# Second attention of a two-attention decoder: maxima subtracted through stack rows, stack halves between spill stages, residual biases later

## Chip, cores and metric

The kernel runs on one core of one Trainium2 chip. The metric is the device time of one execution in microseconds (us). Engines are named as in the profile: PE (TensorE matmul), PEld (its weight loads), DVE (VectorE), ACT (ScalarE), POOL (GpSimd), SP (SyncE); SPq and ACTq are the DMA issues of SP and ACT.

## What is computed

One decoder layer over 16 batches of 128 tokens, width 128, 16 heads of 8 features, post-norm: a first attention with a decayed second score term and mixed values, a layer norm, a second attention whose keys and values come from a context, a layer norm, and a mixture of 16 experts (top 4) with a last layer norm. The part that the change touches:

```python
Q = query @ Wq.T + bq; K = key @ Wk.T + bk; V = value @ Wv.T + bv
energy = jnp.einsum('bhqd,bhkd->bhqk', Q, K) / jnp.sqrt(jnp.float32(HD))
attn = jax.nn.softmax(energy, axis=-1)
x = jnp.einsum('bhqk,bhkd->bhqd', attn, V)
return x.transpose(0, 2, 1, 3).reshape(b, -1, D) @ Wo.T + bo
```

## The kernel before

Every stage works batch by batch. To get float32 scores out of bf16 matmuls, queries and keys are cut into three bf16 parts (`high` and `middle` on ACT, L1216 and L1220; `remainder` and `lowest` on POOL, L498 and L504). SP **spills** the parts to DRAM (L365, L369, L370, L373) and loads them back **stacked** (L396, `stack2`): one bf16 operand holds the 48 part-by-feature rows that a head needs, on the even partitions 0 to 94, for all 16 heads, once for the queries (side 0) and once for the keys (side 1). The other partitions hold zeros. There are four such stacks (`stk2`), laid over the two stacks `stk` of the first attention.

A batch of the second attention then goes through these steps, four heads (a group) at a time. `score2` (L799, four bf16 matmuls) makes scores with the queries in the rows. `maximum2` on DVE (L1529) takes each query's maximum over the keys into `top`. When all 16 heads are done, `turn_top` (L812) transposes `top` into bank 6 and ACT copies it into `top_t`, one row per head (`take_top`, L1245). `score_t` (L821) makes the scores again with the keys in the rows, and four more bf16 matmuls (L828) subtract the maxima from them:

```python
m = pe.matmul(bank[2 + g % 2][:, 128 * j:128 * j + 128],
              neg_ident[:, h:h + 1].broadcast_to([128, 128]), top_t[:, b.par, :],
              start=False, stop=True, skip_group_check=True)
```

ACT exponentiates (`exponent2`, L1236), PE weighs the values (`weigh`, L844), transposes to tokens (`to_tokens`, L857), DVE divides (L1536, L1542), PE turns (L866) and multiplies by the output weights (`out_product`, L870) with ACT's copy between them (`take_out`, L1261), DVE adds residual and bias (`residual`, L1560), takes the moments (L1548 to L1553) and normalises (`norm_out`, L1566) with a power from POOL (L578). The bias of the residual is added to x ahead of time, four batches in one POOL instruction (`residual_bias`, L641).

The order is written out by hand. A **slot** is four units g = 0 to 3; in PE's slot n, unit g does in this order: for g = 0 `project2` of batch n+3 (L751, L752), one group of `score2`, one of `score_t` (batch n-2), at g = 1 and 3 a `weigh`, at g = 1 `turn_out` and at g = 2 `out_product` (batch n-4), at g = 2 `turn_top` (batch n-1), at g = 3 `to_tokens` (batch n-3). ACT, DVE, POOL and SP have the same slots with their own steps. Slots 0 to 3 of the second attention overlap the last steps of the first; in them `last_slot1` gives POOL the first attention's layer norms (`gain_and_sum`, `inverse_root`). In slots 12 to 17 the routing of the first 8 batches is added (`route_first` on PE, `route_stage` on DVE). Slot n starts where `project2` of batch n+3 runs. The experts follow and end at 355.4 us.

Each engine's queue is in order. A step waits for semaphores: `score2` for the stack (`stacked`) and the maximum two groups back (`maxed`), `score_t` for the exponent two groups back (`exped`), `exponent2` for the subtraction (`shifted`), SP's `stack2(b)` for its spill and for the last subtraction of batch b-4, which used the same stack.

## Time and profile before

| | us |
|---|---|
| median of 3 runs (lowest to highest) | 356.3 (355.46 to 356.36) |
| the profiled execution, its own time | 357.19 |
| its span, first to last instruction | 355.4 |
| PE busy, share of the span | 326.9 (92%) |
| DVE busy | 250.7 (71%) |
| POOL busy | 215.4 (61%) |
| ACT busy | 190.7 (54%) |
| mean busy share of the 16 DMA engines by queue: SP's, ACT's | 51.9%, 0.9% |

The profiled execution took 1.8 us more than its span, and stands 0.9 us over the median. Busy is the time in which an engine had an instruction of its own; register, semaphore and DMA-issuing instructions are not counted. A busy share over the whole span says little here, since the stages have different limits; the stage is to be read by itself, in stretches of time and in the order of its instructions. In a timeline row stand the start, the duration, the engine, the line, the operation, out<-in with the shapes, the count of merged instructions, and in brackets the idle time just before with what ended it. The TensorE clock was granted at 0.995 of full speed on average.

### The profile page before, as it was taken

How to read it: one execution, taken by the hardware profiler on the slowest of the kernel's cores; microseconds unless marked ns; L12 is line 12 of the kernel's file. 1: busy time of each engine (PE TensorE's matmuls, PEld its weight loads, DVE VectorE, ACT ScalarE, POOL GpSimd, SP SyncE). 2: the span in 40 equal slices, each digit the busy share in tenths (PEclk: the TensorE clock that was granted, in tenths of full speed). 3: DMA queues.
4: the chain of work that ended last, by engine and by line, in shares of the span. 5: the costliest groups of instructions: out<-in, count | busy, mean ns of one | idle time of the engine just before them, and what ended most of it. 6: DMA issues, size and time to landing. Idle time of an engine off the chain costs nothing.

```text
span 355.4 us, 11656 instructions
## 1 busy us (share of the span) xinstructions
PE 326.9 (92%) x3728; PEld 259.1 (73%) x3728; DVE 250.7 (71%) x1220; ACT 190.7 (54%) x458; POOL 215.4 (61%) x402
## 2 busy tenths in 40 slices
PE   6989899998999999975799999998889999999993
PEld 3877788887888888864588887887646765666662
DVE  1688899988989999966367767769754279254454
ACT  3586566766676665575677767754643342222220
POOL 8375899998889977788733343311134445554552
PEclk9999999999999999999999999999999999999998
DMA  7669797775677688545454544641055300624310
GB/s 219 191 188 307 233 268 229 231 223 166 202 201 208 179 235 236 168 130 140 115 133 115 145 116 99 164 106 46 10 175 183 87 32 7 180 88 144 122 32 30
DMA packets 67808, 54.07 MB, mean 152 GB/s; under 512 B 29617, under 2 KB 57649, under 8 KB 67633
## 3 DMA queue, kind: packets, MB, share of 16 engines
q1 hardware_dynamic: 67328, 52.43, 51.9%
q10 hardware_dynamic: 432, 1.05, 0.9%
q8 instruction: 25, 0.41, 0.5%
q14 instruction: 23, 0.18, 0.2%
HBM read 33.40 MB, written 20.05 MB: 150 GB/s over the span
## 4 chain that ended last, share of the span: by engine, by line
PE 45%; POOL 16%; issue 11%; DVE 9%; DMA 9%; ACT 4%; SPq 4%; POOLq 0%; ACTq 0%; DVEq 0%
PE bank L844 6%; PE bank L1109 5%; DMA parts_dram<-parts 4%; PE bank L1113 4%; PE bank L784 4%; PE bank L1122 4%; DMA stk<-parts_dram 2%; PE bank L773 2%; POOL rstd L562 2%; PE bank L799 2%; POOL rest L498 2%; DMA sup_w<-in_sup_w_dram 2%; PE bank L828 2%; PE bank L821 2%; PE bank L787 2%
## 5 line engine op out<-in xcount | busy, mean ns | idle before, releaser
L707 POOL TENSOR_TENSOR stk<-stk 128x512 f32<-128x512 f32 x32 | 40.8, 1274 | 38.3 <-ACT stk L1434 35.4
L1227 ACT ACTIVATE prob_t<-bank 128x512 f32<-128x512 f32 x64 | 38.7, 605 | 41.6 <-PE bank L787 41.6
L1518 DVE CUSTOM_DVE_ANT_0 sums<-bank,decayed_e 128x128 f32<-128x128 f32 x256 | 59.1, 287 | 0.7
L1529 DVE TENSOR_REDUCE top<-bank 128x4 bf16<-128x512 f32 x64 | 43.9, 687 | 17.2 <-PE bank L799 16.9
L1236 ACT ACTIVATE prob_t<-bank 128x512 f32<-128x512 f32 x64 | 38.8, 606 | 26.7 <-PE bank L828 26.3
L1774 DVE TENSOR_TENSOR stk<-bank,stk 128x512 f32<-128x512 f32 x32 | 22.0, 691 | 39.2 <-POOL stk L707 38.0
L1434 ACT ACTIVATE stk<-bank 128x512 f32<-128x512 f32 x32 | 19.1, 597 | 53.6 <-PE bank L1109 53.6
L1506 DVE TENSOR_TENSOR decayed_e<-bank,decay 128x512 f32<-128x512 f32 x64 | 44.0, 687 | 2.5 <-issue 1.9
L498 POOL TENSOR_TENSOR rest<-pf,parts 128x256 f32<-128x256 f32 (+1 forms) x31 | 28.1, 908 | 28.9 <-ACT parts L1216 28.8
L844 PE MATMUL bank<-prob_t,vmix 128*32 128x128 f32 x1024 | 42.6, 278 | 2.2 <-ACT pvs L1253 2.2
L784 PE MATMUL bank<-ident,sums 128*128 128x128 f32 x256 | 39.3, 276 | 2.7 <-ACT prob_t L1227 1.2
L504 POOL TENSOR_TENSOR parts<-rest,parts 128x256 bf16<-128x256 f32 (+1 forms) x31 | 28.2, 908 | 20.5 <-ACT parts L1220 20.5
L1122 PEld LDWEIGHTS bank<-w,stk 128*128 128x128 f32 x192 | 25.1, 191 | 11.9 <-issue 8.4
L1109 PE MATMUL bank<-x_t,w 128*128 128x512 f32 x64 | 32.9, 595 | 0.0
L1113 PE MATMUL bank<-x_t,w 128*128 128x512 f32 x64 | 32.7, 592 | 0.0
L844 PEld LDWEIGHTS bank<-prob_t,vmix 128*32 128x32 f32 x1024 | 25.7, 109 | 9.4 <-issue 3.9
L784 PEld LDWEIGHTS bank<-ident,sums 128*128 128x128 f32 x256 | 28.0, 141 | 5.8 <-DVE shift L1518 3.5
L763 PE MATMUL bank<-stk 128*128 128x128 bf16 x256 | 24.8, 219 | 1.2 <-DMA stk<-parts_dram 1.2
L1122 PE MATMUL bank<-w,stk 128*128 128x128 f32 x192 | 25.4, 275 | 0.0
L799 PE MATMUL bank<-stk 128*128 128x128 bf16 x256 | 24.9, 220 | 0.4 <-DVE top L1529 0.4
L773 PE MATMUL bank<-stk 128*128 128x128 bf16 x256 | 25.0, 220 | 0.0
L821 PE MATMUL bank<-stk 128*128 128x128 bf16 x256 | 24.8, 219 | 0.0
(171 smaller groups left out, 756.6 us busy)
## 6 DMA issues: line engine op xcount, KB each, us to landing
stk<-parts_dram SPq DMA_DIRECT2D x32, 384.0 KB, 4.3
stk<-shares_dram SPq DMA_DIRECT2D x64, 128.0 KB, 2.9
parts_dram<-parts SPq DMA_DIRECT2D x32, 192.0 KB, 3.5
parts_dram<-parts SPq DMA_DIRECT2D x48, 128.0 KB, 3.1
stk<-parts_dram SPq DMA_DIRECT2D x32, 192.0 KB, 2.9
parts_dram<-parts SPq DMA_DIRECT2D x32, 96.0 KB, 2.3
parts_dram<-parts SPq DMA_DIRECT2D x48, 64.0 KB, 2.1
w<-in_w_dram SPq DMA_DIRECT2D x3, 512.0 KB, 5.6
```

The lines of the kernel that those rows point to most:

```text
L498: pool.tensor_tensor(rest[:, :, L.kinds, :], pf[:, :, L.kinds, :], by_part[b.par][:, HIGH, L.kinds, :], ALU.subtract).then_inc(L.rest, 1)
L707: pool.tensor_tensor(h1[kk % 2], sg[kk % 2], share[kk], ALU.mult).then_inc(weighted, 1)
L784: pe.matmul(bank[3][:, 128 * j:128 * j + 128], sums[g % 2][:, j, :], ident[:], start=(j == 0), stop=True, is_transpose=True, skip_group_ch ...
L844: w = pe.matmul(bank[4][32 * j:32 * j + 32, 128 * m:128 * m + 128], vmix[b.par][:, head(2 * m, j) // 2, e:e + 2, :].rearrange("p e f -> p ...
L1109: pe.matmul(bank[kk % 2][:], w1[:, 128 * kk:128 * kk + 128], xt, start=True, stop=True).then_inc(gate_mm, 1)
L1113: pe.matmul(bank[UP_BANK[u % 3]][:], w3[:, 128 * kk:128 * kk + 128], xt, start=True, stop=True).then_inc(up_mm, 1)
L1122: m = pe.matmul(bank[4 + c % 2][:, 128 * t:128 * t + 128], actt[u % 3][:, 128 * t:128 * t + 128], w2[:, kk, :], start=(kk == 0 and t == 0) ...
L1227: act.activation(prob_t[g][:].rearrange("p h t -> p (h t)"), bank[3][:], ACT.Exp).then_inc(L1.exped, 1)
L1236: act.activation(prob_t[g][:].rearrange("p h t -> p (h t)"), bank[2 + g % 2][:], ACT.Exp).then_inc(L2.exped, 1)
L1506: dve.tensor_tensor(decayed_e[:, g % 2], bank[E_BANK[g % 2]][:].rearrange("p (h t) -> p h t", h=GH), decay[:].unsqueeze(1).broadcast_to([1 ...
L1518: m = dve.tensor_tensor_reduce(out=sums[g % 2][:, j, :], in0=bank[g % 2][:, 128 * j:128 * j + 128], in1=decayed_e[:, g % 2, j, :], scale=1 ...
L1529: dve.tensor_reduce(top[:, b.par, GH * g:GH * g + GH], bank[S2_BANK[g % 2]][:].rearrange("p (h t) -> p h t", h=GH), AX.X, ALU.max).then_in ...
```

## The change

**Rows for the maxima.** The stacks have unused partitions. Rows 96 to 111 of the key side now hold, for head h, minus one in row 96+h and zero in the others (`pick_rows`, two DMAs early in the program; the number in the constant is one whose float32 bits are two bf16 of -1). Rows 96 to 111 of the query side hold all 16 maxima, put there for every head by a DMA that ACT issues (`top_rows`, 16 partitions of 16 copies of 128 bf16, 64 KB). So the four matmuls of `score_t` subtract the maxima too, and those of L828 are gone. `score2` of the next batch in the same stack needs zeros in these rows: POOL clears them (`clear_row`, 16 partitions of 1024 float32), for the 12 batches that have a successor in their stack.

**Order.** `score2` and `maximum2` run three units earlier. `turn_top` moves from unit 2 to unit 3 of the slot before, into bank 4, and `take_top` to ACT's unit 0; `top_rows` follows the exponent of unit 0. SP loads a stack in two halves of 8 heads, both sides in one DMA; a half waits for half of batch b-4's `score_t`, and the halves stand between the three stages of the next batch's spill. `clear_row(b)` opens POOL's slot b+3. The residual biases move from the transition (slots 0 to 3) to the ends of slots 3, 5, 7 and 9. Loops of SP, POOL and DVE over the slots are written out.

```diff
+            def pick_rows(p):
+                sp.wait_ge(zeroed[p], 1)
+                keys = stk[p][:].rearrange("p a h u t -> p (a h u t)").bitcast(F32)[TOP_ROW:TOP_ROW + H, H * S:2 * H * S]
+                sp.dma_start(keys.rearrange("p (k n) -> p k n", k=2),
+                             k["pick_rows"].unsqueeze(1).broadcast_to([H, 2, H * S // 2])).then_inc(in_rows_k, 16)
...
-                for side in range(2):
-                    sp.dma_start(stk2[b.buf][0:2 * R:2, side], src[side]).then_inc(L2.stacked[b.buf], 16)
+                if half == 0:
+                    sp.wait_ge(L2.spilled[b.par], b.pair * L2.spill_step + L2.spill_step)
+                if b.n >= 4:
+                    sp.wait_ge(L2.shifted, NG * b.n - 4 * NG + NM + NM * half)
...
+            for s in range(NB - 2):
+                if s + 3 < NB:
+                    spill_high(L2, slot_batch(s + 3))
+                stack2(slot_batch(s + 2), 0)
+                if s + 3 < NB:
+                    spill_mid(L2, slot_batch(s + 3))
+                stack2(slot_batch(s + 2), 1)
+                if s + 3 < NB:
+                    spill_low(L2, slot_batch(s + 3))
...
+            def clear_row(b):
...
+                pool.wait_ge(L2.shifted, NG * b.n + NG)
+                pool.memset(stk2[b.buf][TOP_ROW:TOP_ROW + H, 0].rearrange("p h t -> p (h t)").bitcast(F32), 0.0
+                            ).then_inc(L2.row_zero, 1)
...
+                c = b.back(3)
+                if c.live and c.n < NB - 4:
+                    clear_row(c)
+                    pool.wait_ge(L2.row_zero, c.n + 1)
...
+            for n in range(1, NB + 4):
+                if n < 4:
+                    last_slot1(NB + 1 + n, None)
                 slot2(slot_batch(n))
+                if n % 2 == 1 and 3 <= n < 11:
+                    residual_bias(2 * n - 6, 2 * n - 2)
...
             def score_t(b, g):
...
+                if g == 0:
+                    pe.wait_ge(L2.topped[b.par], b.pair * 16 + 16)
                 for j in range(GH):
-                    pe.matmul(bank[2 + g % 2][:, 128 * j:128 * j + 128], stk2[b.buf][:, 1, head(g, j), :],
-                              stk2[b.buf][:, 0, head(g, j), :], start=(j == 0), stop=True,
-                              skip_group_check=True)
-                if g == 0:
-                    pe.wait_ge(L2.top_t_ev, b.n + 1)
-                for j in range(GH):
-                    h = GH * g + j
-                    m = pe.matmul(bank[2 + g % 2][:, 128 * j:128 * j + 128],
-                                  neg_ident[:, h:h + 1].broadcast_to([128, 128]), top_t[:, b.par, :],
-                                  start=False, stop=True, skip_group_check=True)
+                    m = pe.matmul(bank[2 + g % 2][:, 128 * j:128 * j + 128], stk2[b.buf][:, 1, head(g, j), :],
+                                  stk2[b.buf][:, 0, head(g, j), :], start=True, stop=True)
...
-                sb_, sg_ = unit_back(bb.back(1), g, -2)
+                sb_, sg_ = unit_back(bb.back(1), g, -5)
...
-                if g == 2 and bb.back(1).live:
-                    turn_top(bb.back(1))
+                if g == 3 and bb.live and (not isinstance(bb.n, int) or bb.n >= 1):
+                    turn_top(bb)
...
+            def top_rows(b):
+                act.wait_ge(L2.top_t_ev, b.n + 1)
+                act.dma_start(stk2[b.buf][TOP_ROW:TOP_ROW + H, 0],
+                              top_t[0:H, b.par, :].unsqueeze(1).broadcast_to([H, H, S])).then_inc(L2.topped[b.par], 16)
...
-                if g == 3 and bb.back(1).live:
+                if g == 0 and bb.back(1).live:
                     take_top(bb.back(1))
...
                 if bb.back(2).live:
                     exponent2(bb.back(2), g)
+                if g == 0 and bb.back(1).live:
+                    top_rows(bb.back(1))
```

The line numbers of the two programs differ: after the change `score2` is L843, `score_t` L865, `weigh` L885, `out_product` L911, the exponent L1283, the row DMA L1288, the clearing L696, the stack L422.

PE, units 2 and 3 of slot 5 (banks 0 and 5 take `score2`, 2 and 3 `score_t`). Before:

```order
L799 MATMUL bank0<-stk1 128x128 [waits maxed2,stacked21]
L799 MATMUL bank0<-stk1 128x128 x3
L821 MATMUL bank2<-stk1 128x128 [waits exped2]
L821 MATMUL bank2<-stk1 128x128 x3
L828 MATMUL bank2<-top_t,neg_ident 128x128 x4
L870 MATMUL bank7<-late_w,attn_ot 128x128 [waits o_t_ev2]
L812 MATMUL bank6<-ident_bf,top 16x128 [waits top_t_ev2,proj_ev2,maxed2]
L799 MATMUL bank5<-stk1 128x128 [waits maxed2]
L799 MATMUL bank5<-stk1 128x128 x3
L821 MATMUL bank3<-stk1 128x128 [waits exped2]
L821 MATMUL bank3<-stk1 128x128 x3
L828 MATMUL bank3<-top_t,neg_ident 128x128 x4
```

Now, the same two units:

```order
L843 MATMUL bank5<-stk1 128x128 [waits maxed2]
L843 MATMUL bank5<-stk1 128x128 x3
L865 MATMUL bank2<-stk1 128x128 [waits exped2]
L865 MATMUL bank2<-stk1 128x128 x3
L911 MATMUL bank7<-late_w,attn_ot 128x128 [waits o_t_ev2]
L843 MATMUL bank0<-stk0 128x128 [waits maxed2,row_zero2,stacked24]
L843 MATMUL bank0<-stk0 128x128 x3
L865 MATMUL bank3<-stk1 128x128 [waits exped2]
L865 MATMUL bank3<-stk1 128x128 x3
```

Two groups of L828 are gone from these two units and four from the slot; the first group of a new batch stands in unit 3, where it waits for the cleared row and for the first half of its stack, and the transpose stands behind the `weigh` that follows these rows.

ACT, from the exponent of unit 0 to `take_out` in unit 1, inside its loop. Before:

```order
L1236 ACTIVATE prob_t0<-bank2 128x512 [waits pv2]
L1193 ISA
L1198 ACTIVATE pf<-bank6,bias_q 128x128 [waits rest2,proj_done2]
L1201 ACTIVATE pf<-bank6,first_w 128x128
L1231 REGISTER_ALU
L1236 ACTIVATE prob_t1<-bank3 128x512 [waits pv2,shifted2]
L1211 ISA
L1215 REGISTER_ALU [waits proj_ev2]
L1216 CAST parts0<-pf 128x2x128 [waits spilled20]
```

Now:

```order
L1296 COPY top_t<-bank4 16x128 [waits topped20]
L1278 ISA
L1280 ISA [waits shifted2]
L1283 ACTIVATE prob_t0<-bank2 128x512 [waits pv2]
L1288 DMA stk0<-top_t 16x16x128 [waits top_t_ev2]
L1240 ISA
L1245 ACTIVATE pf<-bank6,bias_q 128x128 [waits rest2,proj_done2]
L1248 ACTIVATE pf<-bank6,first_w 128x128
L1278 REGISTER_ALU
L1283 ACTIVATE prob_t1<-bank3 128x512 [waits pv2,shifted2]
```

The copy of the maxima has moved ahead of the slot's first exponent, and a DMA issue stands between that exponent and the projection.

SP, one slot's worth. Before, one stack and then one whole spill:

```order
L396 DMA stk1<-parts2_dram 48x2048 x2
L365 DMA parts2_dram<-parts0 128x3x128 x2
L369 DMA parts2_dram<-parts0 128x2x128
L370 DMA parts2_dram<-parts0 128x2x128
L373 DMA parts2_dram<-parts0 128x2x128
```

Now:

```order
L376 DMA parts2_dram<-parts1 128x3x128 x2
L422 DMA stk0<-parts2_dram 48x2x1024
L384 DMA parts2_dram<-parts1 128x2x128
L385 DMA parts2_dram<-parts1 128x2x128
L422 DMA stk0<-parts2_dram 48x2x1024
L392 DMA parts2_dram<-parts1 128x2x128
```

Seven issues have become seven; the stack of one batch is threaded between the stages of the next batch's spill.

## Rows read from the trace of the kernel before

**Rows 1.** Stretches: us; busy PE, PEld, DVE, ACT, POOL; clock, DMA share, GB/s

```profile
154.70:177.20 22.50, 14.98 (x219) 12.09 (x216) 12.45 (x38) 14.35 (x39) 18.83 (x46) 1.00 0.49 119
177.72:183.46 5.74, 5.70 (x92) 4.71 (x91) 3.86 (x11) 4.44 (x12) 1.94 (x3) 1.00 0.42 103
217.86:223.67 5.81, 5.70 (x93) 4.70 (x91) 4.20 (x13) 4.06 (x12) 2.08 (x4) 1.00 0.46 120
223.67:229.59 5.92, 5.92 (x96) 5.08 (x95) 4.21 (x13) 4.49 (x13) 2.08 (x4) 1.00 0.67 163
229.59:236.78 7.19, 7.19 (x109) 6.37 (x107) 4.33 (x13) 3.55 (x9) 2.02 (x4) 1.00 0.49 122
235.00:259.60 24.60, 21.88 (x355) 17.93 (x354) 19.18 (x75) 12.41 (x29) 3.69 (x8) 1.00 0.19 54
```

**Rows 2.** Timeline of PE, from the start of slot 7 to that of slot 8

```profile
194.93 0.39 PE L751 MATMUL bank<-x_t,late_w 128*128 128x128 f32 x2
...
195.60 0.39 PE L821 MATMUL bank<-stk 128*128 128x128 bf16 x4
...
195.82 0.39 PE L828 MATMUL bank<-top_t,neg_ident 128*128 128x128 bf16 x4
...
198.44 0.49 PE L870 MATMUL bank<-late_w,attn_ot 128*128 128x128 f32 x2
...
198.86 0.22 PE L812 MATMUL bank<-ident_bf,top 128*16 128x128 bf16 x1
...
200.66 0.39 PE L751 MATMUL bank<-x_t,late_w 128*128 128x128 f32 x2
```

**Rows 3.** Timeline of ACT in the same slot: first exponent, copy for the output product

```profile
196.32 0.60 ACT L1236 ACTIVATE prob_t<-bank 128x512 f32<-128x512 f32 x1 [1.27 <-PE bank L828]
...
198.09 0.30 ACT L1261 COPY attn_ot<-bank 128x128 f32<-128x128 f32 x1
```

**Rows 4.** Timelines of POOL, DVE and PE in the transition, slots 2 to 4

```profile
164.79 1.27 POOL L641 TENSOR_TENSOR xb_all<-x_tok,rows 128x512 f32<-128x512 f32 x1
...
167.04 0.29 DVE L1596 BATCH_NORM_STATS2 stats<-res 128x6 f32<-128x128 f32 x1 [2.27 <-POOL res L573]
...
167.98 0.22 PE L812 MATMUL bank<-ident_bf,top 128*16 128x128 bf16 x1 [2.24 <-DVE top L1529]
...
177.23 0.66 PE L1001 MATMUL bank<-ident,x_tok 128*128 128x128 f32 x4 [0.92 <-ACT x_tok L1272]
```

**Rows 5.** Timeline of DVE, slots 14 to 17: ends of its full stretch

```profile
237.20 0.69 DVE L1529 TENSOR_REDUCE top<-bank 128x4 bf16<-128x512 f32 x1 [2.04 <-PE bank L799]
...
254.45 0.39 DVE L1745 TENSOR_TENSOR shares<-vsz,rsm 128x128 f32<-128x128 f32 x1
```

**Rows 6.** The page, DMA issues: KB each, median us from issue to landing

```profile
stk<-parts_dram SPq DMA_DIRECT2D x32, 192.0 KB, 2.9
...
parts_dram<-parts SPq DMA_DIRECT2D x48, 64.0 KB, 2.1
```

**Rows 7.** SP's stack of L396: landings of all, and one issue of two DMAs

```profile
DMA to landing us min/median/max: 2.7/2.9/4.3
...
201.06 1.29 SPq L396 DMA_DIRECT2D stk<-parts_dram  x2
```

**Rows 8.** Start of the program: POOL clears both stacks, ACT issues a DMA

```profile
0.73 6.96 POOL L483 MEMSET stk<- 128x4096 f32 x2 [0.29 <-POOLq L1903]
...
1.66 0.45 ACTq L1190 DMA_DIRECT2D x_t<-in_x_t_dram  x1
```

**Rows 9.** DVE's normalisation alone in slot 7, and beside a POOL instruction later

```profile
197.49 0.34 DVE L1566 TENSOR_SCALAR c_tok<-res,mv,rstd 128x128 f32 x1
...
263.39 1.26 POOL L707 TENSOR_TENSOR stk<-stk 128x512 f32<-128x512 f32 x1
...
263.46 1.28 DVE L1566 TENSOR_SCALAR c_tok<-res,mv,rstd 128x128 f32<-128x128 f32 x1 [0.18 <-POOL rstd L578]
```

More of the change, by code:

```diff
@@ L236, in __init__ @@
                 self.spilled = [sem(f"spilled{n}{p}") for p in range(2)]
-                self.stacked = [sem(f"stacked{n}{p}") for p in range(4)]
+                self.stacked = [sem(f"stacked{n}{p}") for p in range(4 * n)]
                 self.ent_scores = sem(f"ent_scores{n}")
@@ L323, in build @@
         RT_STEPS = 22
+        TOP_ROW = 96
         WARM = 10
@@ L350, in load_ffn, with spill_places @@
                 sp.dma_start(w2[:].rearrange("p c n -> p (c n)"), k["w2"]).then_inc(in_ffn, 16)
-            def spill(L, b):
+            def spill_places(L, b):
                 if L is L1:
@@ L406, in _ @@
             spill(L1, Batch(0, 0))
-            sp.wait_ge(zeroed[0], 1)
+            pick_rows(0)
             stack1(Batch(0, 0), 0)
@@ L410, in _ @@
             spill(L1, Batch(0, 1))
-            sp.wait_ge(zeroed[1], 1)
+            pick_rows(1)
             stack1(Batch(0, 1), 0)
@@ L425, in _ @@
             pair1(NB // 2 - 1)
-            def quad2(q):
-                for i4 in range(4):
-                    b = Batch2(q, i4)
-                    stack2(b)
-                    if b.back(-1).live:
-                        spill(L2, b.back(-1))
-            spill(L2, Batch2(0, 0))
-            load_ffn()
-            quad2(0)
-            with sp.Fori(1, 3) as q:
-                quad2(q)
-            quad2(3)
+            spill(L2, slot_batch(0))
+            load_ffn()
+            spill(L2, slot_batch(1))
+            stack2(slot_batch(0), 0)
+            stack2(slot_batch(0), 1)
+            spill(L2, slot_batch(2))
+            stack2(slot_batch(1), 0)
+            stack2(slot_batch(1), 1)
+            for s in range(NB - 2):
[7 more added lines that the diff above has]
+                    spill_low(L2, slot_batch(s + 3))
             def spill_shares(half):
@@ L906, in unit2 @@
                     project2(bb.back(-3))
-                sb_, sg_ = unit_back(bb.back(1), g, -2)
+                if g == 0 and isinstance(bb.n, int) and bb.n == 0:
+                    score2(bb, 0)
+                sb_, sg_ = unit_back(bb.back(1), g, -5)
                 if sb_.live:
                     score2(sb_, sg_)
+                if g == 0 and isinstance(bb.n, int) and bb.n == 1:
+                    turn_top(bb.back(1))
                 tb = bb.back(2)
@@ L1065, in route_first @@
                     turn_shares(0, 1)
+            pe.wait_ge(in_rows_k, 16)
             first_slot()
+            pe.wait_ge(in_rows_k, 32)
             pair1(1)
@@ L1647, in unit2 @@
                     residual(L2, bb.back(4), TAIL2)
-                sb_, sg_ = unit_back(bb.back(1), g, -2)
+                if n == 0 and g == 0:
+                    maximum2(bb, 0)
+                sb_, sg_ = unit_back(bb.back(1), g, -5)
                 if sb_.live:
@@ L1751, in scan @@
                 rstep(dve.tensor_tensor(r[dst][:, :, sh:NE], r[src][:, :, sh:NE], r[src][:, :, 0:NE - sh], ALU.add))
-            dve.wait_ge(xb2, 1)
-            slot2(slot_batch(4))
-            dve.wait_ge(xb2, 4)
-            with dve.Fori(1, 3) as q:
-                for i4 in range(1, 5):
-                    slot2(Batch2(q, 0).back(-i4))
-            for n in range(13, NB + 3):
+            for n in range(4, NB + 3):
                 slot2(slot_batch(n))
@@ L1895 @@
                                    v["L0_ffn_gate_w"].T], 1),
+        "pick_rows": _np.repeat(-1.0058441162109375 * _np.eye(H), S // 2, 1),
         "x_t": turned(v["x"]),
```

113 lines of the change are left out of this document (61 added, 52 removed).

## The prediction, made blind

> **What bounds the kernel now.** I read the stretches first (busy time of each engine by stage), then PE's, ACT's and DVE's timelines in the second attention, and last what SP's queue and its landings leave over.
>
> The stretches [rows 1] show three kinds of stage. In slots 4 to 11 (177.72 to 223.67, eight slots in 45.95 us, 5.74 each) PE is busy 5.70 of 5.74; DVE has 4.2, ACT 4.1, POOL 2.1. PE is the bound there, and slots 12 and 13 (5.92 and 7.19 us) are fully PE's. In the transition (154.70 to 177.20) PE has 15.0 of 22.5 us and POOL 18.8: POOL bounds it, through the first attention's layer norms. In 235.00 to 259.60 DVE has the most work beside the routing, and its timeline has no gap from 237.20 to the end of the shares at 254.84 [rows 5].
>
> Inside a PE slot [rows 2] a group of four bf16 matmuls costs 0.22 us (195.60 to 195.82). The one real wait is before L870: it follows ACT's copy at 198.09 [rows 3] by 0.35. So a second chain is hidden just under PE's: the group of L828 at 195.82, the exponent at 196.32 (0.50 later), ACT's in-order work to the copy at 198.09 (1.77 more), L870 at 198.44, then the rest of PE's slot, 2.22 us to 200.66. This chain closes on itself once per slot, since the next slot's first `score_t` comes behind it on PE.
>
> **The slots 4 to 11.** The change takes four groups of L828 from each slot, 0.89 us of PE work. If PE alone decided, a slot would be 4.85. But only two of the groups lie on the chain: the one before the first exponent (0.22) and the one after L870 (0.22); the other two lie where PE waits for L870 anyhow. Besides, L812 stood 0.42 behind L870 because it waited for DVE's last maximum; it now comes later in the slot, with all maxima three units earlier, which gives some 0.1 back. A slot becomes 5.74 - 0.22 - 0.22 - 0.1 = 5.20.
>
> The DMA that ACT now issues stands inside this chain, between the exponent and the projection. The nearest row is ACT's issue at the start, 0.45 us [rows 8]. Below is nothing: the exponent runs 0.60 us and the next ACT instruction starts 0.5 behind it, so an issue by ACT's sequencer may fit beside it. Above is 0.45. I take 0.1, as the order of the two favours the overlap: slot 5.30, eight slots save 8 x 0.44 = 3.5 us. Bounds: 0.7 (slot 5.65) to 4.3 (5.20).
>
> What covers the rest. *The row DMA* moves 64 KB. It is issued about 1.7 us after the slot's start and needed by the next slot's `score_t`, 0.66 after that starts, so 4.2 us later. The nearest row by size lands in 2.1 us, SP's stacks of 192 KB in 2.9, the slowest in 4.3 [rows 6, 7]. I take 2.1 to 2.9: hidden. The Trainium skill, SBUF — State Buffer, section "Door 1: The DMA port swizzle", says that a transfer's rate depends on the SBUF ports its partitions reach, and gives 16 adjacent partitions 4 ports, about 109 GB/s. By that, an estimate, the 64 KB would take 0.6 us beside the fixed part instead of 0.15, and land near 2.6; the sum stays the same. No row of this trace has so few partitions.
>
> *The clearing* is 1024 elements; POOL cleared 2 x 4096 in 6.96 us, 0.85 us per 1024 [rows 8]. POOL has 3.6 us free per slot, and the row is needed only in unit 3 of that slot: nothing on the path. Four later bias pieces (1.27 each [rows 4]) bring a slot of POOL to 2.1 + 0.9 + 1.3 = 4.3, still under 5.3. But POOL's power, which DVE's normalisation waits for, now stands behind both; DVE has 1 us of slack per slot. I allow nothing, and up to 0.5 in three slots in the range. DVE's normalisation took 0.34 alone and 1.28 where it ran beside a POOL instruction of 1.26 [rows 9]. The Trainium skill, SBUF — State Buffer, section "SBUF: two separate sides", calls the port pair of VectorE and GpSimd an exclusive lock held for the whole instruction; the row agrees. By that rule a normalisation that meets a bias piece loses up to 0.9, in three slots 2.7; by rows it waits for the power behind that piece and so cannot meet it.
>
> *The stacks* are needed three groups earlier. Before, a stack was issued in one piece (1.29 us of SP for the pair, at 201.06 [rows 7]) after the last `score_t` of batch b-4. Now a half needs only half of that batch, which is two units earlier, and does not queue behind a whole spill. With 2.9 us to land, the first half of batch b comes about 1.4 us before unit 3 of slot b-1. DVE's load per slot is unchanged, 4.2 of 5.3.
>
> **The transition.** DVE waited 2.27 us for POOL's sum and PE 2.24 for DVE's maximum [rows 4]. POOL's queue ran full, and three bias pieces, each holding it 1.22, stood ahead of work that DVE waited for: 3.7 us. Against it: the first clearing (0.9) stands in slot 3 ahead of the remainder, whose middle part ACT makes before the last x1 row that PE waits for at 177.23 [rows 4]; and DVE takes three more maxima in slot 0 and `score2` of batch 1 may wait for its stack, some 0.6 together. Net 2.2. Bounds: 0 (another chain of the layer norms takes over) to 3.7.
>
> **Slots 12 to 17.** Slots 12 and 13 keep the same chain and PE's extra work: 0.7 each, 1.4 (bounds 0.8 to 1.8). In slots 14 to 16 DVE is full, so PE's saving is worth nothing there; but three of the ten maxima in the full stretch have moved to slots before it, at 0.6 apiece (0.69 long [rows 5], the next started 0.6 later): 1.8 (1.2 to 2.1). In slot 17 the last batch loses its four groups on the way to the last exponent: 0.5 (0.2 to 0.9).
>
> **The start.** `pick_rows` adds two loads of 128 KB behind the first two spills on SP's queue. Their issue lies in SP's wait for the spill, but the bytes go ahead of the first stacks: 0.4 lost (0 to 1).
>
> **Sum.** 3.5 + 2.2 + 1.4 + 1.8 + 0.5 - 0.4 = 9.0 us less. The profiled execution took 357.19 (span 355.4), so it would take 348.2, with a span of 346.4. The median of the runs is 0.9 lower than that execution: 356.3 - 9.0 = 347.3. The experts after 259.6 only shift.
>
> **Rivals.**
> 1. *The issue counts in full.* ACT's DMA issue does not overlap the exponent: slot 5.65, the eight slots give 0.7 and slots 12 and 13 some 0.4 less: gain 5.8, 350.5 us. For it: ACT's other instruction at the start came right behind its issues. Against: nothing then ran on ACT's datapath. Chance 0.15.
> 2. *The stacks or POOL decide.* SP has seven issues per slot (0.37 to 0.65 each) and a spill's landing of 2.1 between the last issue and the next half, near 5 us, barely under the slot; contention would set the slot at 5.5: 8 x 0.2 less than forecast, and another 1 in slot 0: gain 6.4, 349.9. Chance 0.11. With it go cases where two or three small terms fail together and 353 is reached, 0.04.
> 3. *The rows come late, and it is slower.* The place is `score_t` of unit 0. The loop is: group, exponent 0.5 later, issue 0.5 later, landing L, PE 0.1: slot = L + 1.1. It passes 5.30 at L = 4.2 and the old 5.74 at 4.6. For: the transfer shares the engines with SP's 192 KB halves; the slowest of those took 4.3 [rows 7]; DMA engines are about half busy [rows 1]. Against: the median is 2.9 for three times the bytes. At L = 5.2 the slot is 6.3: slots 4 to 11 lose 8 x 0.56 = 4.5, slot 12 loses 0.4, slot 13 gains 0.7, slots 14 to 16 (16.9 us before) lose 2.0, transition, slot 17 and start keep 2.3: 3.9 slower, 360.2. It decides from L = 4.85. Chance 0.09. The Trainium skill, DMA: Bandwidth & Descriptors, section "Issuing engines are not separate DMA queues", says that DMAs of all engines run on the same 16 and interleave, so ACT's own queue would not shield the rows. This trace has ACT's queue only at the start and cannot show it.
>
> **The numbers.** Forecast 0.61, the rivals 0.15, 0.15 (with the small failures) and 0.09. A measurement of this kernel tells about 0.3%, 1.1 us, from no change. The forecast's own bounds are 343.5 (most terms at their high end: 12.8) to 351 (the issue, the transition and slots 12 to 17 at their low ends); rivals 1 and 2 and the failures reach to 353.5; the late rows are left out. Range 343.5 to 353.5. Faster 0.87, same 0.04, slower 0.09.
>
> **What the new profile would show.** Slots 4 to 11 at 5.2 to 5.4, with PE idle before L911 and its releaser ACT's copy; the idle time before `score_t` (L865) small. ACT's row DMA landing in 2 to 3 us. The projection 0.5 to 0.6 behind the slot's first exponent (rival 1: 0.9 or more). No idle time before L843 on a stack or a cleared row (rival 2). Slot 4 starting at about 175.9, DVE's full stretch about 15.8 long. A PE wait for the row DMA in every slot, or slots near 6, would make the prediction wrong.

## The result, and the profile after

The changed kernel takes 353.94 us (median; 351.20 to 357.83, 20 executions); the kernel before took 357.63 in the executions beside it. The ratio is 0.9881, 95% interval 0.9857 to 0.9904: 4.2 us faster, not 9.0. (Ratios here leave out executions more than 1.5% above the fastest of their kernel, five of the twelve of e11 for one; medians do not, and so the two can differ.) The profiled execution took 354.09 with a span of 352.3, 3.1 less than the 355.4 before. The stretches after, from slot 1 to the experts; the columns are those of [rows 1]:

```profile
157.25:176.52 19.27, 13.65 (x161) 11.21 (x160) 10.31 (x31) 11.76 (x32) 14.65 (x38) 0.88 0.59 147
176.52:182.79 6.27, 5.63 (x75) 4.80 (x75) 3.56 (x10) 4.45 (x12) 2.47 (x4) 0.82 0.40 98
176.52:222.02 45.50, 38.65 (x593) 31.31 (x593) 33.02 (x94) 32.35 (x89) 27.59 (x42) 0.98 0.59 142
222.02:228.02 6.00, 5.57 (x87) 4.59 (x86) 4.47 (x15) 4.72 (x14) 3.26 (x6) 1.00 0.76 174
228.02:234.52 6.50, 5.95 (x86) 5.08 (x84) 4.12 (x12) 3.58 (x8) 3.70 (x6) 1.00 0.44 110
234.52:256.41 21.89, 18.66 (x263) 13.71 (x262) 17.57 (x71) 12.03 (x28) 3.06 (x7) 0.84 0.14 42
```

PE's work fell as planned (38.65 us in slots 4 to 11), but those slots still take 45.50. Against the forecast, by stage:

| stage | before | forecast | after |
|---|---|---|---|
| start of slot 1 | 157.86 | 158.3 | 157.25 |
| slots 1 to 3 | 19.86 | 17.7 | 19.27 |
| slots 4 to 11 | 45.95 | 42.4 | 45.50 |
| slots 12, 13 | 13.11 | 11.7 | 12.50 |
| slot 14 to the experts | 22.84 | 20.5 | 21.89 |
| experts to the end | 95.78 | 95.8 | 95.89 |

Slot 1 began anywhere from 157.25 to 161.00 in the profiled executions of all kernels here, so the first row is scatter. The clock row of the page (40 slices of 8.8 us) of the changed kernel shows dips that were absent before, where it read 9 in every slice but the last:

```profile
PEclk9999999999999999998989999999699999999998
```

And PE's timeline where slot 4 begins:

```profile
173.64 0.38 PE L843 MATMUL bank<-stk 128*128 128x128 bf16 x4 [3.35 <-POOL stk L696]
...
175.62 1.11 PE L1046 MATMUL bank<-ident,x_tok 128*128 128x128 f32 x4 [0.40 <-ACT x_tok L1323]
176.52 0.63 PE L788 MATMUL bank<-x_t,late_w 128*128 128x128 f32 x2
176.95 0.63 PE L789 MATMUL bank<-c_t,late_w 128*128 128x128 f32 x2
177.38 0.63 PE L843 MATMUL bank<-stk 128*128 128x128 bf16 x4
177.80 0.63 PE L865 MATMUL bank<-stk 128*128 128x128 bf16 x4
```

Some 2 us behind a wait of 3.35 us a group of four starts every 0.43 us instead of 0.22: TensorE runs at its lower level, 1.2 GHz, not 2.4. Slots 5, 7 and 9 are clean (no bias piece and no lower clock in them): 5.37, 5.36, 5.37. Slot 4 took 6.27, slots 6, 8 and 10 took 5.74, 5.63 and 6.15, slot 11 5.61, slot 3 8.98 (8.22 before).

ACT in a clean slot, and behind it the landing times of its DMAs:

```profile
206.07 0.60 ACT L1283 ACTIVATE prob_t<-bank 128x512 f32<-128x512 f32 x1 [1.12 <-PE bank L865]
206.09 0.59 ACTq L1288 DMA_DIRECT2D stk<-top_t  x1
206.88 0.37 ACT L1245 ACTIVATE pf<-bank,bias_q 128x128 f32<-128x128 f32 x1 [0.22 <-issue]
...
DMA to landing us min/median/max: 2.4/3.3/4.9
```

The projection starts 0.81 behind the exponent, where 0.5 was usual: the issue runs beside the exponent, but outlasts the point at which the next instruction could start. The landing, 3.3 against the 2.1 to 2.9 assumed, made PE wait nowhere. The Trainium skill, SBUF — State Buffer, "Door 1: The DMA port swizzle", led to an estimate of 2.6. The trace agrees within its scatter: the smallest landing was 2.4, and the median was 3.3 here but 2.6 in the repeat of the same kernel (e15). SP's 64 KB spills also went from 2.1 [rows 6] to 2.6, which would fit other transfers in the way, but that was not tried:

```profile
parts_dram<-parts SPq DMA_DIRECT2D x48, 64.0 KB, 2.6
```

POOL and DVE in slot 8, one of those with a bias piece:

```profile
200.07 1.27 POOL L672 TENSOR_TENSOR xb_all<-x_tok,rows 128x512 f32<-128x512 f32 x1
201.40 0.95 POOL L696 MEMSET stk<- 16x1024 f32 x1
202.43 0.55 POOL L609 TENSOR_TENSOR rstd<-veps,minus_half 128x1 f32<-128x1 f32 x1
202.95 0.67 POOL L529 TENSOR_TENSOR rest<-pf,parts 128x256 f32<-128x256 f32 x1
...
203.01 0.69 DVE L1619 TENSOR_SCALAR c_tok<-res,mv,rstd 128x128 f32<-128x128 f32 x1 [1.11 <-POOL rstd L609]
203.62 0.68 DVE L1581 TENSOR_REDUCE top<-bank 128x4 bf16<-128x512 f32 x1
```

The power stands behind piece and clearing; DVE waits 1.11 for it, then its normalisation takes 0.69 instead of 0.34 [rows 9] beside POOL's remainder, and the last maxima, which PE's L854 needs, come late.

### The profile page after: what moved, and what is told of

It reads as the page before. It is cut to its first block, busy times and chain, and to the rows that moved or that the text cites. A ratio compares the mean times of both kernels' runs of the same rounds, so it can differ in the third digit from the quotient of the medians.

```text
span 352.3 us, 11006 instructions
## 1 busy us (share of the span) xinstructions
PE 317.4 (90%) x3472; PEld 248.7 (71%) x3472; DVE 250.3 (71%) x1219; ACT 189.9 (54%) x458; POOL 226.7 (64%) x414
## 4 chain that ended last, share of the span: by engine, by line
PE 52%; issue 11%; DMA 10%; ACT 9%; DVE 8%; SPq 4%; POOL 3%; ACTq 1%; POOLq 0%; DVEq 0%
PE bank L885 7%; PE bank L821 6%; DMA parts_dram<-parts 5%; PE bank L1156 4%; PE bank L1160 4%; PE bank L1169 4%; PE bank L810 4%; DMA stk<-parts_dram 3%; PE bank L824 3%; PE bank L780 3%; PE bank L800 2%; PE bank L898 2%; PE bank L865 2%; PE bank L911 2%; DMA sup_w<-in_sup_w_dram 2%
## 5 line engine op out<-in xcount | busy, mean ns | idle before, releaser
L1283 ACT ACTIVATE prob_t<-bank 128x512 f32<-128x512 f32 x64 | 38.6, 605 | 23.9 <-PE bank L865 23.0
L885 PE MATMUL bank<-prob_t,vmix 128*32 128x128 f32 x1024 | 43.4, 283 | 2.2 <-ACT pvs L1304 2.2
L885 PEld LDWEIGHTS bank<-prob_t,vmix 128*32 128x32 f32 x1024 | 26.2, 111 | 9.5 <-issue 4.0
L843 PE MATMUL bank<-stk 128*128 128x128 bf16 x256 | 25.7, 226 | 5.0 <-POOL stk L696 3.3
L865 PE MATMUL bank<-stk 128*128 128x128 bf16 x256 | 26.6, 231 | 0.6 <-ACT prob_t L1283 0.6
L800 PE MATMUL bank<-stk 128*128 128x128 bf16 x256 | 24.8, 219 | 1.0 <-DMA stk<-parts_dram 0.9
L843 PEld LDWEIGHTS bank<-stk 128*128 128x128 bf16 x256 | 19.8, 105 | 7.4 <-issue 4.0
```

The lines of the kernel that those rows point to most:

```text
L843: m = pe.matmul(bank[S2_BANK[g % 2]][:, 128 * j:128 * j + 128], stk2[b.buf][:, 0, head(g, j), :], stk2[b.buf][:, 1, head(g, j), :], start= ...
L885: w = pe.matmul(bank[4][32 * j:32 * j + 32, 128 * m:128 * m + 128], vmix[b.par][:, head(2 * m, j) // 2, e:e + 2, :].rearrange("p e f -> p ...
L1283: act.activation(prob_t[g][:].rearrange("p h t -> p (h t)"), bank[2 + g % 2][:], ACT.Exp).then_inc(L2.exped, 1)
```

## The experiments

All were measured as above, in ratio to the kernel before on the same chip; runs on different chips are compared by these ratios. "Chg" in the tables is the changed kernel as profiled first, e15 the same kernel again: the two rows show how far one profiled execution can be from another. Slot times are from the one profiled execution of each kernel, and so are subject to that execution's clock.

| run | median us | ratio (95%) |
|---|---|---|
| e1_fill | 352.63 | 0.985 (0.9808 to 0.9891) |
| e2_clear0 | 352.96 | 0.9861 (0.9814 to 0.9908) |
| e3_no_rows | 351.70 | 0.9807 (0.975 to 0.9864) |
| e4_no_clears | 350.11 | 0.9786 (0.9745 to 0.9827) |
| e5_rows96 | 352.02 | 0.9784 (0.9734 to 0.9833) |
| e6_turn | 351.25 | 0.9806 (0.9757 to 0.9855) |
| e7_bias_back | 355.80 | 0.9925 (0.99 to 0.9951) |
| e8_rows_pool | 351.06 | 0.9816 (0.9782 to 0.9851) |
| e9_all | 354.71 | 0.9878 (0.983 to 0.9925) |
| e10_all_fill | 353.90 | 0.988 (0.984 to 0.9921) |
| e11_whole | 357.77 | 0.9937 (0.99 to 0.9974) |
| e12_hybrid | 350.52 | 0.9774 (0.9726 to 0.9822) |
| e13_hybrid_fill | 350.82 | 0.9815 (0.9758 to 0.9873) |
| e14_turn_fill | 350.77 | 0.9817 (0.9761 to 0.9874) |
| e15_changed | 354.15 | 0.988 (0.983 to 0.993) |

| us | slots 1-3 | slot 3 | slot 4 | slots 5, 7, 9 | slots 6, 8, 10 | slots 4-11 | slot 12 to experts |
|---|---|---|---|---|---|---|---|
| before | 19.86 | 8.22 | 5.74 | 5.73 5.73 5.74 | 5.74 5.73 5.73 | 45.95 | 35.95 |
| chg | 19.27 | 8.98 | 6.27 | 5.37 5.36 5.37 | 5.74 5.63 6.15 | 45.50 | 34.39 |
| e1 | 18.51 | 9.01 | 5.41 | 5.38 5.35 5.37 | 5.78 5.64 5.64 | 43.93 | 33.00 |
| e2 | 18.33 | 8.82 | 6.71 | 5.37 5.35 5.37 | 5.75 5.65 5.63 | 45.87 | 34.54 |
| e3 | 19.07 | 9.76 | 5.90 | 5.05 5.04 5.05 | 5.64 5.64 5.63 | 43.07 | 33.11 |
| e4 | 17.59 | 8.09 | 5.41 | 5.40 5.35 5.38 | 5.69 5.40 5.94 | 43.92 | 37.96 |
| e5 | 17.85 | 7.33 | 5.42 | 5.37 5.35 6.31 | 5.71 6.71 5.43 | 45.66 | 36.05 |
| e6 | 15.28 | 5.85 | 5.60 | 5.61 5.57 5.38 | 5.18 5.39 5.91 | 43.82 | 32.66 |
| e7 | 22.63 | 10.96 | 6.27 | 5.38 5.36 5.37 | 5.75 5.39 5.43 | 44.30 | 32.80 |
| e8 | 19.54 | 8.35 | 5.05 | 5.04 5.40 5.33 | 5.14 5.14 5.23 | 42.14 | 33.60 |
| e12 | 17.14 | 6.52 | 5.18 | 5.50 5.06 5.48 | 5.56 5.41 5.35 | 42.60 | 35.55 |
| e15 | 19.22 | 9.73 | 6.27 | 5.38 5.35 5.37 | 5.79 5.64 5.76 | 44.96 | 36.33 |

**e1, the clock.** Matmuls on zeros ahead of PE's longest waits (24 in slot 3 as below, and 4 and 7 in slot 1, 5 and 8 in slot 15):

```diff
 def score2(b, g):
+    if u == 4 * NG:
+        pe.wait_ge(L2.maxed, u - 1)
+        fill(S2_BANK[0], 24)
```

> The changed kernel with 48 matmuls of 256 bf16 columns on zeros (about 0.11 us each at the full clock) put on TensorE ahead of its longest waits: 4 and 7 in slot 1, 24 in slot 3 ahead of the scores that wait 3.35 us for the first clearing, 5 and 8 in slot 15; nothing is taken out. Theory A (part of the missing gain is the halved TensorE clock behind the idle stretches): the granted clock of 160 to 180 us and 240 to 260 us goes from 0.81-0.85 to about 1.00, slot 4 from 6.27 to about 5.4 us, and the run is 1.5 to 3 us shorter than the changed kernel (351 to 352.5 beside 353.9). Rival B (the stretches at half the clock lie in slack, waits for POOL, ACT and DVE set the end): the clock returns to 1.00 but the time stays within 0.7 us of the changed kernel, or grows by what the added matmuls overshoot their waits.

The same two stretches of before, of the changed kernel and of e1:

```profile
160.00:180.00 20.00, 13.85 (x216) 11.75 (x216) 10.43 (x30) 12.14 (x32) 15.47 (x37) 1.00 0.54 135
240.00:260.00 20.00, 17.28 (x284) 13.57 (x284) 16.38 (x67) 10.56 (x26) 2.84 (x6) 1.00 0.12 39
```

```profile
160.00:180.00 20.00, 15.15 (x181) 12.88 (x182) 9.63 (x27) 12.82 (x36) 13.96 (x33) 0.83 0.54 132
240.00:260.00 20.00, 17.00 (x196) 11.55 (x194) 14.02 (x59) 11.18 (x24) 3.05 (x7) 0.83 0.16 54
```

```profile
160.00:180.00 20.00, 16.60 (x213) 13.61 (x212) 10.82 (x32) 12.50 (x35) 15.27 (x39) 1.00 0.59 146
240.00:260.00 20.00, 17.00 (x214) 11.38 (x212) 14.75 (x61) 11.30 (x24) 3.80 (x8) 1.00 0.16 48
```

The clock is back at its upper level; slot 4 falls from 6.27 to 5.41 and the stretch behind slot 12 from 34.39 to 33.00. All six executions had a granted clock of 0.994 to 0.997 and lay within 2.1 us (chg: 0.971 to 0.993, within 6.6). The whole is 1.3 us shorter by the medians, but the intervals overlap: that the waits bring the lower level is shown for this kernel, the net gain of filling them is not. Among the 20 executions of the changed kernel the three at 0.993 took 351.2 to 352.0 us, the five at 0.977 or less 354.1 to 357.8. The mean clock does not explain the whole spread: executions at 0.979 took 351.50 and 356.33, and one of e15 at 0.994 took 356.37. The Trainium skill, TensorE: Matmul & The Clock Gate, "HAM oscillation — how this bites in real kernels", says that waits between bursts of matmuls bring the throttled state back and that the matmuls behind the wait pay; slot 4 agrees.

**e2, the first clearing's place.**

```diff
 for n in range(1, NB + 4):
+    if n == 3:
+        clear_row(slot_batch(0))
     if n < 4:
         last_slot1(NB + 1 + n, None)
```

> The changed kernel with one clearing moved: that of the first stack goes on POOL ahead of the last step of the first attention's layer norms, where POOL now waits 1.1 us for DVE, not behind it. Theory C (in slot 3 TensorE waits 3.35 us for a 0.95 us clearing only since it is queued behind that step, which itself waits for DVE): the wait falls to under 1 us, slot 3 from 8.98 to 6.5 to 7 us, and the run is 2 to 3 us shorter than the changed kernel. Rival D (the last layer norm is the chain that ends slot 3, the clearing only shows first): the wait moves to the transposes of x1 or to ACT, the run is shorter by 0.5 us or less, or longer by up to 0.9 us, since the clearing now delays the layer norm.

```profile
172.78 0.38 PE L845 MATMUL bank<-stk 128*128 128x128 bf16 x4 [2.37 <-DVE top L1583]
...
175.57 1.12 PE L1048 MATMUL bank<-ident,x_tok 128*128 128x128 f32 x4 [1.20 <-ACT x_tok L1325]
```

Rival D. The clearing gave way to DVE's maximum, which stands behind DVE's wait for POOL's layer-norm sum, and then to the last x1. Slot 3 keeps 8.82, and slot 4 was at the lower clock again.

**e3, the issue on ACT.** Without the row DMAs and their waits; the maxima are not subtracted.

```diff
-    if g == 0 and bb.back(1).live:
-        top_rows(bb.back(1))
```

> The changed kernel without ScalarE's 16 DMAs that fill the rows of maxima, and without the two waits for them; the maxima are thus not subtracted. Theory E (the 0.59 us issue holds up the instructions behind it on ScalarE by about 0.3 us in each slot, and ScalarE's queue sets the slot): the projection starts 0.5 us behind the exponent's start, not 0.81, the undisturbed slots fall from 5.37 to 5.1-5.2 us, and the run is 1.5 to 3 us shorter than the changed kernel. Rival F (the issue lies beside the exponent, the slot is set elsewhere, as by DVE and the waits for scores): slots stay at 5.3 to 5.4 us and the run within 0.7 us.

```profile
202.69 0.60 ACT L1281 ACTIVATE prob_t<-bank 128x512 f32<-128x512 f32 x1 [0.92 <-PE bank L863]
203.19 0.36 ACT L1243 ACTIVATE pf<-bank,bias_q 128x128 f32<-128x128 f32 x1
```

Theory E: the projection is 0.50 behind the exponent again and clean slots fall from 5.37 to 5.05, a little further than expected. The issue costs 0.32 a clean slot. Slots 6, 8 and 10 fall only to 5.64, 5.64 and 5.63, so a second chain stands just behind this one there: in slot 6 DVE waits 1.11 us for POOL's power, queued behind bias piece and clearing, as in slot 8 above.

**e4 and e5, the clearings.** e4 drops them, so that rows of an earlier batch stay in the scores from which the maxima are taken. e5 computes what the changed kernel does, since those scores read rows 0 to 95 only:

```diff
-    m = pe.matmul(..., stk2[b.buf][:, 0, head(g, j), :],
-                  stk2[b.buf][:, 1, head(g, j), :], ...)
+    m = pe.matmul(..., stk2[b.buf][0:TOP_ROW, 0, head(g, j), :],
+                  stk2[b.buf][0:TOP_ROW, 1, head(g, j), :], ...)
```

> The changed kernel without the 12 clearings of the stack rows and without the waits for them; the rows of an earlier batch thus stay in the scores of a later one. Theory C (the first clearing's queue place costs slot 3 some 2 us or more, and bias piece plus clearing on POOL, 2.2 us, cost slots 4, 6, 8 and 10 some 0.3 us each by a late rstd or remainder): slot 3 falls to about 6.5 us, slots 6, 8 and 10 to about 5.4, and the run is 3 to 4.5 us shorter than the changed kernel. Rival G (POOL has room in each slot; what ends slot 3 is the last layer norm): under 1 us shorter.

> The changed kernel without the 12 clearings, and with the scores that the maxima are taken from multiplied over stack rows 0 to 95 only, so that the rows of maxima at 96 to 111 are not in them and need no clearing; what is computed stays as it is. Theory C (the clearings' places on POOL are the cost, as the run without clearings showed: slot 3 8.98 to 8.09, slots 8 and 10 from 5.63 and 6.15 to 5.4): a matmul of 96 contracted rows takes as long as one of 128, so the time is that of the run without clearings, 350 to 351 us, 3 us below the changed kernel. Rival: fewer rows in a matmul count for less activity and the granted clock falls more often, 352 us or more.

Both intervals lie wholly below the changed kernel's 0.9857 to 0.9904, and the two ratios are the same: the clearings cost 1% of the time, some 3.4 us (1.7 to 5.1 with the intervals of e4 and of the changed kernel). Slots 1 to 3 gave 1.4 to 1.7, slot 4 0.9 (with no 3.35 us wait ahead of it, it ran at the upper level), slots 8 and 10 where undisturbed 0.2. Slot 3 fell less than expected (8.09 and 7.33, not 6.5), and slot 6 stayed at 5.7. The profiled executions of both had a granted clock of 0.971 and lost behind slot 12 (37.96, 36.05), so their own totals say less than the ratios. A group of 96-row matmuls took the same 0.22.

**e6, the order in slots 2 and 3.** e5, with

```diff
-    slot2(slot_batch(3))
-    turn_x1(3)
-    for n in range(4, 12):
+    for n in range(2, 12):
         slot2(slot_batch(n))
+        if n == 5:
+            turn_x1(3)
```

the copy on ACT moved alike, and on DVE `unit2` ahead of `unit1` in slots 2 and 3. To place that copy, ACT's loop over slots 4 to 11 is written out, a third difference that the expectation does not name:

```diff
-    with act.Fori(1, 3) as q:
-        for i4 in range(4):
-            slot2(Batch2(q, i4))
+    for n in range(4, 12):
+        slot2(slot_batch(n))
+        if n == 5:
+            take_chunk(3, 1, turn1, turn1_ev)
```

> The run with 96 rows and without clearings, and two orders changed: the transposes of the last quarter of x1 on TensorE and their copy on ScalarE go behind slot 5 (their values are first read by the projection of slot 9), and VectorE takes the maxima of slots 2 and 3 ahead of the layer-norm steps of the same unit. Theory H (slot 3 is ended by the last layer norm, through TensorE's place for these transposes and through maxima queued behind VectorE's wait for POOL): slot 3 falls from 8.1 to 5.5-6.5 us, and the run is 1.5 to 2.5 us below the 96-row run, 348 to 349 us. Rival I (the stacks' DMAs are next: the 2.02 us wait for a stack in slot 3 of the run without clearings stays): slot 3 stays above 7 us and the gain is under 0.8 us.

```profile
171.46 0.40 PE L836 MATMUL bank<-stk 96*128 96x128 bf16 x4 [0.74 <-DMA stk<-parts_dram]
...
PEclk9999999999999999999999999999999999999999
```

Theory H for the stretch: slots 1 to 3 take 15.28, slot 3 5.85, and the profiled execution (span 345.7, clock 0.998) never left the upper level. Which of the two orders gave it, no run tells. But the ratio is no better than e5's, and the 1.5 to 2.5 us did not come. Its executions went from 347.51 at 0.998 to 353.42 at 0.980: what it saved showed only where the clock held.

The written-out loop shows on ACT, here in slot 6:

```profile
185.64 0.60 ACT L1275 ACTIVATE prob_t<-bank 128x512 f32<-128x512 f32 x1 [0.17 <-PE bank L858]
186.34 0.37 ACT L1237 ACTIVATE pf<-bank,bias_q 128x128 f32<-128x128 f32 x1
```

The projection stands 0.70 behind the exponent, not 0.81, with the issue still on ACT, and slots 6 and 11 took 5.18, not 5.37. e14, which has the same loop, repeats both (0.70; 5.18 and 5.17). Neither the 96 rows nor the missing clearings shorten a clean slot (e5: 5.37), so what is left is the loop's own instructions on ACT, some 0.19 a clean slot; no run has this difference alone. Slots 4, 5 and 7 of e6 took 5.57 to 5.61, and slot 10 5.91; these were not followed up, but for slot 5, which has the transposes of x1.

**e7, the bias pieces back.**

```diff
+    if n < 5:
+        residual_bias(4 * n - 4, 4 * n)
...
-    if n % 2 == 1 and 3 <= n < 11:
-        residual_bias(2 * n - 6, 2 * n - 2)
```

> The changed kernel with the four bias pieces of 1.27 us back where they stood before, one ahead of each of the last layer-norm steps; all else as changed. Theory J (the later pieces did take 2 to 3 us out of slots 1 to 3, but each now stands in one piece with a clearing and costs 0.27 us in slots 6, 8 and 10): slots 6, 8 and 10 fall to 5.36, the stretch from slot 1 to slot 4 grows by 2 to 3.5 us, the run is 1 to 2.5 us longer than the changed kernel (355 to 356.5). Rival K (slots 1 to 3 wait for the stacks and layer norms anyway): the stretch grows by under 1 us and the run stays within 0.7 us of 353.9.

Theory J: slots 1 to 3 grow by 3.36, PE's wait for the first clearing from 3.35 to 4.83 us, and slots 8 and 10 fall to 5.39 and 5.43. So the later pieces were worth some 3.4 us there in these profiles, and each pair of piece and clearing costs 0.25 later. By the ratios the whole run is 1.6 us longer, with intervals that meet at 0.990. Slot 6 stayed at 5.75, against the expectation.

**e8 to e10, rows issued by POOL.** e8 is e5 with `top_rows` at the head of POOL's slot. e9 adds e6's orders and puts the bias pieces behind POOL's power; e10 adds e1's matmuls of slots 1 and 15, without those of slot 3.

```diff
 def slot2(b):
+    if b.back(1).live:
+        top_rows(b.back(1))
```

> The 96-row run with the DMAs that fill the rows issued by POOL, which has no clearings any more, instead of ScalarE. Theory E (the issue on ScalarE costs 0.3 us in each slot, as the run without rows showed: slots 5.37 to 5.05): slots fall to about 5.05 to 5.15 us and the run is 2 to 2.5 us below the 96-row run. Rival L (the issue takes POOL longer than ScalarE, a microsecond or more, or the rows land later than 5 us, so that the remainder or the scores wait): slots stay at 5.3 or grow, up to 3 us longer in all.

> The changed kernel with all that the runs so far pointed to: scores for the maxima over 96 rows and no clearings, rows issued by POOL, the last quarter of x1 transposed and copied behind slot 5, VectorE's maxima of slots 2 and 3 ahead of the layer-norm steps, and the later bias pieces put where POOL waited 1.2 us for the high parts. If the causes add: slots 4 to 11 at 5.05-5.15 us (as with rows on POOL), slot 3 at 5.5-6 us (as with the late transposes), so some 1.5 to 2 us below the late-transposes run at the same clock: 349 us median, 344 to 345 where the clock holds. If they do not add (the slot is then bound by SP's spill and stack issues, about 6 waits a slot on DMA): slots 5.3-5.6, 351 us or more.

> The run before with the added matmuls on zeros in slots 1 and 15 (4, 7, 5 and 8, 24 in all) that held the clock in the changed kernel. Theory A (a busier TensorE ahead of the feed-forward stage keeps the full clock): granted clock 0.99 or more in nearly every execution, median 1 to 3 us below the run without them, and less scatter. Rival B (the clock falls anyway, now in slots 4 to 11, where TensorE idles more for being faster): the clock of the executions stays spread over 0.97 to 0.99 and the median within 1 us.

PE in e9, the rows it waited for in slots 2, 3 and 4:

```profile
165.67 0.40 PE L865 MATMUL bank<-stk 128*128 128x128 bf16 x4 [1.95 <-DMA stk<-top_t]
...
173.44 0.58 PE L865 MATMUL bank<-stk 128*128 128x128 bf16 x4 [2.00 <-DMA stk<-top_t]
...
181.10 0.38 PE L865 MATMUL bank<-stk 128*128 128x128 bf16 x4 [1.82 <-DMA stk<-top_t]
```

In e8 the slots fell to 5.04 to 5.14 where undisturbed, slot 6 too, and slots 4 to 11 to 42.14, next to the forecast's 42.4. The whole was no shorter than e5, against the expectation: slots 1 to 3 took 19.54 (e5 17.85), with waits of 0.57 and 1.35 us for rows and the clock at 0.65 to 0.67 from 160 to 170. e9 (rows above) has more of it: there too POOL issues the rows behind its layer norms, and PE waited three times, 5.8 us in all, and paid in the clock (0.63 in 170 to 180). e9 and e10 are no better than the changed kernel; neither the 349 us nor e10's steady clock came (0.976 to 0.993 over its executions).

**e11, whole stacks.** SP's order as before:

```diff
-    spill_high(L2, slot_batch(s + 3))
     stack2(slot_batch(s + 2), 0)
-    spill_mid(L2, slot_batch(s + 3))
     stack2(slot_batch(s + 2), 1)
-    spill_low(L2, slot_batch(s + 3))
+    spill(L2, slot_batch(s + 3))
```

> The changed kernel with SP's order as before: both halves of a stack ahead of the whole next spill instead of between its stages. The forecast took the halves to be 1.4 us early in each slot and worth nothing by themselves. Theory M (the stack is early enough either way): within 0.7 us of the changed kernel, waits for stacks about 3.8 us in all as now. Rival N (the scores now run five units ahead, so the stack is wanted earlier and SP's place decides): if the halves between the stages were what made them land in time, TensorE waits for stacks 0.3 to 1 us in most slots and the run is 2 to 6 us longer; if they are what holds up the spill's mid and low stage, it is up to 1.5 us shorter.

What TensorE's scores (weight loads and matmuls together) waited for, first in e11, then in the changed kernel; us in all, times:

```profile
  DMA stk<-parts_dram: 9.8, 11
```

```profile
  DMA stk<-parts_dram: 3.8, 9
```

These lines count a wait twice where weight load and matmul wait for the same stack. The matmuls alone waited 4.3 us in e11 and 1.4 in the changed kernel, so 3 us more, not 6, and the "3.8 us in all" of the expectation is a double count too. Slot 8 took 7.52 (a wait of 0.96 us, then the lower clock), and the ratio went from 0.988 to 0.9937, with intervals that meet at 0.990. Rival N: the halves between the stages are what brings the stacks in time. The waits show it; the 2 us of the whole run are at the edge of the noise.

**e12 to e15, do the causes add?** e12 is e9 with the rows of the first four batches left on ACT. e13 is e12, e14 is e6, each with 24 added matmuls in slots 1 and 15. e15 is the changed kernel again.

```diff
-    if g == 0 and bb.back(1).live:
+    if g == 0 and bb.back(1).live and bb.back(1).n < 4:
         top_rows(bb.back(1))
```

> The kernel with all causes mended, but with the rows of the first four batches issued by ScalarE and those of the other twelve by POOL, since in the run with all rows on POOL TensorE waited three times for rows that POOL issued late in slots 1 to 3, behind the layer-norm steps (5.8 us in all). If that is what spoilt it: slot 3 at 5.5-6.2, slots 5 to 11 at 5.0-5.3 us, median 2.5 to 4 us below the changed kernel. If the causes still do not add: slots of 5.4 or more, within 2 us of the changed kernel.

> The run before with the 24 added matmuls in slots 1 and 15. Theory A: granted clock 0.985 or more in most executions, median 1 us or more below the run without them, less scatter. Rival B: the clock falls anyway, the median within 0.7 us.

> The late-transposes run (rows on ScalarE, 96-row scores, no clearings) with the 24 added matmuls. Its own runs went from 347.5 us at a granted clock of 0.998 to 353.4 at 0.980. Theory A: 0.99 or more in most executions and a median of 348 to 349.5 us. Rival B: the clock stays spread, the median 350.5 to 352.

> The changed kernel itself, as reference on this chip: 353.9 us, ratio to the kernel before 0.988, as on record; granted clock of the executions between 0.97 and 0.993.

e15 repeats the result. In e12 PE waited for no row, so it was POOL's late issue that spoilt slots 1 to 3 of e9; slot 3 took 6.52 and slots 5 to 11 5.06 to 5.56, both longer than expected, and the median came as expected. e12 has the lowest ratio of all, 0.9774, 1.1% below the changed kernel, with intervals apart; from e5 it cannot be told. The added matmuls kept the profiled executions at 0.995, yet e13 and e14 gained nothing: neither theory A's shorter time nor, fully, its steady clock came (0.976 to 0.997 over the executions).

## Why the prediction was wrong

The direction was right and the time was not: half of the gain came. The upper end of the range was also added up wrong. With the issue, the transition and slots 12 to 17 at their low ends the gain is 0.7 + 0 + 2.2 - 0.4 = 2.5, which gives 353.8 us, not the 351 stated, and 354.4 with the start at its low end.

- **The chain of a slot: right, its size partly by luck.** The slots with nothing else in them took 5.36 to 5.38, forecast 5.30, with PE idle before L911 for ACT's copy as said. Inside, two errors cancelled: "an issue by ACT's sequencer may fit beside it ... I take 0.1" measured 0.32, and the slot without it is 5.05, not 5.20. Rival 1 saw the cost but put it on the wrong base. The loop on ACT, which e6 suggests to be part of both figures (5.18 without it), was not in the forecast.
- **"POOL's power ... now stands behind both; ... I allow nothing": the step that failed in slots 4 to 11.** I compared POOL's sum per slot (4.3) with the slot, and not the place of one short instruction in its order. Slots 8 and 10 lost 0.25 each by it (e7, e4), and the clearing of slot 3 held PE 3.35 us. Slot 6 lost 0.37 and has two causes, each enough by itself. One is this power: without rows the slot still takes 5.64 (e3). The other is ACT's issue, which begins 0.33 behind the exponent there and 0.02 in slot 5, so that the projection stands 1.14 behind: without the bias piece the slot still takes 5.75 (e7). With the clearing gone and the issue off ACT it takes 5.14 (e8), and in e6, where the issue begins at once, 5.18. ACT's issue begins there while one of SP's runs; that SP holds it up was not tried.
- **The clearing, "nothing on the path", and 0.9 for the first: mis-sized.** All clearings together cost some 3.4 us (e4, e5). In slot 3 it is not its 0.95 that counts: it is queued behind the last layer norm, and that waits for DVE. Moved ahead, it gives way to DVE's maximum and the last x1 (e2).
- **The transition.** The later bias pieces gave 3.4 of the 3.7 forecast (e7). Gone again were 1.4 to 1.7 to the clearings and 0.8 to the clock (e1); the two may overlap. What ends slot 3 is x1's last quarter and DVE's late maxima: e6 moved both, and slot 3 fell to 5.85.
- **The clock: no step at all.** Every term took PE's durations as given. The change made PE idle more, and waits brought the lower level in slot 2, from the end of slot 3 into slot 4, and in slots 16 and 17. By e1's profile this was 0.8 in slots 1 to 3, 0.9 in slot 4 and 1.4 behind slot 12, about 3 us of the profiled execution. Where the level falls differs from one execution to the next: the repeat e15 kept the upper level in slot 2, lost it from the wait of slot 3 on (3.60 us) and took 36.33 from slot 12 to the experts, 1.9 more than the first profile. Behind slot 12 the forecast was 3.7 less; 1.6 came, 2.95 with the clock held.
- **Rows landing late: rightly unlikely.** The landings reached 4.9 but PE waited for none while ACT issued them. The halves earn their place (e11), which I had counted as cover only.

From slot 1 to the experts the forecast is 9.4 less; the changed kernel gave 2.6, e1 with the clock held 6.3. The remaining 3.1 are 0.85 in slots 1 to 3 (e5, without clearings, is there within 0.2 of the forecast), 0.54 in slots 8 and 10, 0.41 in slot 6, 0.07 in each of the eight slots, and 0.75 behind slot 12. Of the last, 0.35 are in slots 12 and 13, where e1's PE waited 0.45 for a stack, and 0.4 behind them, where DVE's full stretch took 16.2 us (235.14 to 251.33), not 15.8. How the clock's falls are spread over executions, and why the repaired kernels e6, e13 and e14 do not keep it, stays open.

## What to carry to other kernels

When a step is put on an engine with room to spare, ask what short instruction will now stand behind it and who waits for that; the sum of busy time does not tell. A clearing could be avoided here by reading fewer rows, at the same matmul time (0.22 us for a group of 96 rows or of 128). A loop on an engine whose in-order work lies in the slot's chain is worth writing out as a trial of its own (e6). And a cut in the bounding TensorE's work can open waits that bring its lower clock: compare the clock row before counting a gain.
